# The low part of the transposed probabilities between the row maxima of two heads, in the first attention of a fused attention and mixture-of-experts kernel

## What is computed

```python
x = L0_attn_x
x = x + _layernorm(_L0_attn_ref(_layernorm(x, axis=-1), L0_attn_Wq, L0_attn_Wk, L0_attn_Wv, L0_attn_Wo), axis=-1)
x = x + _layernorm(_L0_ffn_ref(_layernorm(x, axis=-1), ...), axis=-1)

# in _L0_attn_ref
scores = jnp.einsum('bhqd,bhkd->bhqk', q, k) * scale
causal = jnp.tril(jnp.ones((T, T), dtype=bool))
scores = jnp.where(causal, scores, -jnp.inf)
attn = jax.nn.softmax(scores, axis=-1)
out = jnp.einsum('bhqk,bhkd->bhqd', attn, v)
out = out.transpose(0, 2, 1, 3).reshape(B, T, D)
return out @ Wo.T
```

## Time and profile before

| | |
|---|---|
| median of 3 runs | 939.19 us (936.19 to 939.78) |
| profiled execution, device time | 939.04 us |
| its span | 937.1 us |
| first attention, first scores to last projection | about 27.7 to 175 us of the span |
| busy in the whole span | PE 863.4 us (92%), DVE 616.3 (66%), ACT 567.0 (61%), POOL 456.4 (49%) |
| granted TensorE clock, mean | 0.98 of full speed |

### The profile page before, as it was taken

How to read it: one execution, slowest core, us unless ns; L and a number is a source line. 1 busy time by engine, 2 the same in 40 slices (tenths; PEclk the granted TensorE clock), 3 DMA queues, 4 the chain that set the end, 5 groups by cost and what they waited for, 6 DMA issues and landing times. The chain is left out here.

```text
span 937.1 us, 18767 instructions
## 1 busy us (share of the span) xinstructions
PE 863.4 (92%) x6108; PEld 799.0 (85%) x6108; DVE 616.3 (66%) x1620; ACT 567.0 (61%) x1570; POOL 456.4 (49%) x486
## 2 busy tenths in 40 slices
PE   5799997769999999999999999969999999999994
PEld 4699987668989989999889999858888888888884
DVE  5466768667787788877887777664545545454456
ACT  6889888656767776667676676654334343333333
POOL 3734334277677776677677777610222212222121
PEclk9999999998999999999999999997999999999997
DMA  7000000051124111411111111101433333333321
GB/s 238 1 22 27 22 23 1 23 147 35 34 61 122 47 40 40 136 46 45 36 35 46 45 37 47 41 1 41 150 107 102 116 117 100 112 101 117 118 79 45
DMA packets 50246, 63.34 MB, mean 68 GB/s; under 512 B 5728, under 2 KB 36064, under 8 KB 50176
## 3 DMA queue, kind: packets, MB, share of 16 engines
q1 hardware_dynamic: 49088, 61.41, 22.4%
q10 hardware_dynamic: 1088, 1.05, 0.3%
HBM read 41.86 MB, written 1.18 MB: 46 GB/s over the span
## 5 line engine op out<-in xcount | busy, mean ns | idle before, releaser
L639 POOL TENSOR_TENSOR b_prob<-b_prob,b_rsum 128x256 f32<-128x256 f32 (+1 forms) x128 | 104.8, 840 | 104.3 <-DVE b_rsum L621 104.3
L73 PE MATMUL banks<-act_t,b_w 128*128 128x256 f32 (+1 forms) x392 | 129.5, 330 | 4.4 <-DVE b_work L1203 3.3
L74 PE MATMUL banks<-act_t,b_w 128*128 128x256 f32 (+1 forms) x392 | 127.4, 325 | 0.0
L75 PE MATMUL banks<-act_t,b_w 128*128 128x256 f32 (+1 forms) x392 | 127.1, 324 | 0.0
L1965 ACT ACTIVATE moe_hid<-banks 128x512 fp32r<-128x512 f32 x66 | 39.5, 598 | 124.6 <-DVE banks L2056 124.6
L1364 ACT ACTIVATE b_prob<-banks,b_negmax 128x128 f32<-128x128 f32 (+1 forms) x256 | 103.6, 416 | 12.6 <-DVE b_negmax L1351 12.5
L2049 DVE TENSOR_TENSOR moe_gated<-banks,moe_share 128x512 f32<-128x512 f32 x66 | 45.6, 691 | 85.1 <-PE banks L75 81.2
L1220 ACT ACTIVATE b_qt<-b_work 128x512 fp32r<-128x512 f32 x64 | 40.5, 632 | 97.5 <-POOL b_work L1215 97.5
L1215 POOL TENSOR_TENSOR b_work<-b_work 128x512 f32<-128x512 f32 x64 | 88.1, 1377 | 9.2
L639 POOL TENSOR_TENSOR a_prob<-a_prob,a_rsum 128x256 f32<-128x256 f32 x64 | 52.4, 840 | 75.5 <-DVE a_rsum L621 75.3
L1211 POOL TENSOR_TENSOR b_work<-b_work,rope_t 128x512 f32<-128x512 f32 x64 | 83.2, 1299 | 7.2 <-DMA b_work<-b_work 7.2
(11 more groups left out here) (237 smaller groups left out, 3019.1 us busy)
## 6 DMA issues: line engine op xcount, KB each, us to landing
b_work<-b_work SPq DMA_DIRECT2D x128, 128.0 KB, 2.3
moe_share<-gates SPq DMA_DIRECT2D x32, 512.0 KB, 3.6
b_w_raw<-in_b_wq SPq DMA_DIRECT2D x4, 1024.0 KB, 5.5
b_w_raw<-in_b_wo SPq DMA_DIRECT2D x4, 1024.0 KB, 9.0
a_src_t<-act_t SPq DMA_DIRECT2D x5, 512.0 KB, 3.0
moe_w_raw<-in_wg SPq DMA_DIRECT2D x16, 128.0 KB, 2.1
moe_w_raw<-in_wu SPq DMA_DIRECT2D x16, 128.0 KB, 2.2
moe_w_raw<-in_wd SPq DMA_DIRECT2D x16, 128.0 KB, 2.2
```

What stands on the lines that cost most here:

```text
L73: nc.tensor.matmul(out, w_lo, m_hi, start=start, stop=False, skip_group_check=skip)
L74: nc.tensor.matmul(out, w_hi, m_lo, start=False, stop=False, skip_group_check=skip)
L75: return nc.tensor.matmul(out, w_hi, m_hi, start=False, stop=stop, skip_group_check=skip)
L639: last = self.m.nc.gpsimd.tensor_tensor(rows, rows, rsum[:, :, t:t + 1].to_broadcast([PART, 2, width]), ALU.mult)
```

## The change

The class of the first attention gets its own `slot_dve`. In it `dve_max` is called once per head, and `dve_prob_t` stands between the two calls. The calls that did nothing in this class (`dve_queries`, late units) are left out. Each call of `dve_max` has the wait on `exp_done` that was there once per slot. The second attention keeps the old `slot_dve`.

```diff
@@ -604,10 +604,10 @@
-    def dve_max(self, dve, p, P):
+    def dve_max(self, dve, p, P, heads=(0, 1)):
         nc, m = self.m.nc, self.m
         wait(dve, self.exp_done, 2 * P - 2)
-        for h in range(2):
+        for h in heads:
             wait(dve, self.s_full, 2 * P + 1 + h)
@@ -706,6 +706,28 @@
 class AttentionA(Attention):
+
+    def slot_dve(self, dve, it, p, units=True):
+
+
+        now = self.stage(it, p, 0)
+        if now:
+            self.dve_max(dve, *now[1:], heads=(0,))
+        if prob := self.stage(it, p, 3):
+            self.dve_prob_t(dve, *prob[1:])
+        if now:
+            self.dve_max(dve, *now[1:], heads=(1,))
+        if before := self.stage(it, p, 1):
+            self.dve_normalise(dve, *before[1:])
+        if out := self.stage(it, p, 4):
+            self.dve_outputs(dve, *out)
+        u = self.early_unit(p, units)
+        if u is not None:
+            self.dve_unit(dve, it + 1, u)
+        if now and p == PAIRS - 1:
+            self.dve_values(dve, it)
+        if p == 0 and not (isinstance(it, int) and it < 2):
+            self.dve_add(dve, it - 2)
```

## The result

The changed kernel takes 942.47 us (median of 11 runs, 940.85 to 947.25) against 939.04 for the kernel before beside it. The ratio is 1.0056, its 95% interval 1.0043 to 1.007: slower by 5.3 us (4.0 to 6.6), an interval that also holds the 4.7 us under which no change can be told. The two medians by themselves lie 3.4 us apart. Forecast were 5.45 us and 944.7 us, in a range of 941.4 to 948.4. The profiled execution took 942.47 us.

What follows compares the result with a forecast made beforehand. TensorE was taken to bound the first attention's middle, with something else at its end. Filling 0.5, iterations 3.15 and end 1.8 sum to +5.45 us over 939.04: 944.5, forecast as a 944.7 us median, range 941.4 to 948.4.

Steps and rivals of the forecast that it cites:

- a loop of VectorE and ScalarE: Steady middle of the first attention: the lengthened loop takes 17.31 us per iteration against TensorE's 16.46; chance 0.78.
- Full cover: Rival: the middle stays bound by TensorE, only filling and end cost 0.5 + 1.8, 941.5 us; chance 0.12.
- No effect: Rival: the low part L645 still runs when it did, since something else released it, 939.2 us; chance 0.02.
- the term of +3.15: Iterations 2 to 5 in the middle: 0.6 us for the first, then three of 0.85.
- the 0.26: First of iterations 2 to 5: ScalarE's wait at TensorE, 0.26 us, is used up before the full 0.85 shows.
- The end: Behind the loop: head 1's exponentials about 0.6 us later in slots 25, 26 and 31, together +1.8 us.
- my division by slots: Behind the loop: +0.59 in slot 25, repeated in 26, nothing in 27 to 30, +0.60 in slot 31.
- The filling: Slots 3 to 7: head 1's exponentials start 0.49 us later and pass it on in full, +0.5 us.
- L645 starts at 40.92 as before, because it had waited for L582: In the filling: the low part gets no earlier start, so head 1's exponentials move from 42.01 to 42.50.
- The extra waits: Each slot's added wait on `exp_done`, plus a register instruction in the loop's 16 slots: taken as nothing, at most +2.7 us.
- Faster: Rival: behind the loop L520 is released earlier eight times by 0.53 us, −4.2, so 935.0 us; chance 0.05.
- VectorE holds longer: Rival: in the new order VectorE's instructions hold their whole duration, 1.3 us more per iteration, 951 us; chance 0.03.

Runs made afterwards that it cites:

- e1: The kernel before with head maxima in two calls, old order, so only the extra wait and register instruction are added; ratio 0.9991 to before.
- e2: The change's new order only in iterations 0 to 5, iterations 6 and 7 as in the kernel before; ratio 1.0035 to before.
- e3: The change's new order only in iterations 6 and 7, the others as in the kernel before; ratio 1.0016 to before.
- e6: The change, with VectorE's add L654 moved ahead of the unit in slot p = 0; middle 66.64 us, ratio 1.0037 to before.
- e4: The change, but with the low part L645 ahead of both heads' maxima; middle 76.40 us, ratio 1.0203 to before.
- e10: The change itself measured and profiled once more, against the kernel before; middle 68.32 us, ratio 1.0052.
- e5: The change with L645 split: 384 columns between the two heads' maxima, 384 behind them; middle 66.50 us, ratio 1.0002 to before.
- e7: The kernel before with add L654 ahead of the unit and LayerNorm statistics of slots 24 and 25 moved into gaps; ratio 0.9981.
- e8: The kernel before, old order, with only add L654 moved ahead of the unit; end 52.20 us, ratio 0.9983.

## Why the prediction was right

The mechanism that was forecast is the one that the runs show. That the total of 5.45 us lies so near the 5.3 of the runs is in part luck: by the profiles the terms came out as −0.22, +2.50 and +2.01 where I had 0.5, 3.15 and 1.8.

- **The core, a loop of VectorE and ScalarE that outgrows TensorE's 16.46 us**: shown. e1 excludes the rest of the edit; e2 and e3 tie the middle's cost to the middle's order; e6 takes 0.60 out of the loop and 0.54 per iteration comes back, down almost to TensorE's own time; e4 puts more in and the iterations grow as summed. *Full cover* and *No effect* fall with the middle of 68.35.
- **Its size**: the term of +3.15 was too large, 2.50 measured. The iterations cost 0.27, 0.67, 0.90 and 0.66 where I had 0.6 and three times 0.85. The first counts for half of the difference; the pipeline seems to enter the loop with more slack than the 0.26 that I took from ScalarE's wait, which I didn't trace. For the others 17.31 was summed and 17.21 measured on average. The hand-over from the maxima to the exponentials is one reason (105.56 − 104.92 = 0.64 against my 0.71).
- **The end**: +1.8 forecast, +2.01 measured. Head 1's exponentials come 2.05 and 2.04 behind the first maximum (2.11 forecast) in slots 25 and 31. From slot 23 to slot 31 it is 39.11 us against 37.89, +1.22 for the 1.2 of slots 25 and 26; what follows is +0.79 for 0.6. But e2 shows that 0.7 of it belongs to the order in slot 23 and before, and e3, with the new order behind the loop alone, takes 38.41 us from slot 23 to slot 31, only 0.52 more than before. So my division by slots is right in its sum only, by luck.
- **The filling** was wrong: +0.5 forecast, −0.22 measured in the change's profile, −0.22 in e6's and −0.23 in e10's. The step that failed is "L645 starts at 40.92 as before, because it had waited for L582". It fits the profile that it was read from, but the block starts in one of two ways. In six profiles (the change, e2, e5, e6, e7, e10) its first scores come 7.2 to 7.4 us behind the block's first memset, in the other seven, the kernel before among them, 8.24 us. The eight matmuls just ahead of those scores, in e7, then in e8:

```profile
24.78 1.04 PE L826 MATMUL banks<-ident,b_w 128*128 128x128 f32 x8
```

```profile
25.33 1.91 PE L822 MATMUL banks<-ident,b_w 128*128 128x128 f32 x8
```

All six early profiles have 1.04 us there, all seven late ones 1.91 or 1.92. What decides it isn't known; the order of the low part doesn't, since e7 and e8 both have the old order in the filling. With the late start L645 does have to wait for L582: e4 puts it ahead of all maxima, and it starts 21.46 us behind the memset, against 21.50 before. With the early start L582 comes 0.58 us sooner (20.03 us behind the memset, against 20.61), and L645 can move. Kernel after, DVE and PE in the filling, answering:

```profile
39.69 0.95 DVE L645 TENSOR_TENSOR a_prob_t<-banks,a_prob_t 128x768 fp32r<-128x768 f32 x1
...
40.79 0.85 PE L520 MATMUL banks<-ident,a_prob 128*128 128x128 f32 x6 [0.50 <-DVE a_prob_t L645]
43.67 0.36 PE L73 MATMUL banks<-a_prob_t,b_w 128*128 128x256 f32 x1 [0.55 <-DVE b_w L920]
```

e7 has the old order there, and the same early start:

```profile
40.38 0.95 DVE L645 TENSOR_TENSOR a_prob_t<-banks,a_prob_t 128x768 fp32r<-128x768 f32 x1
...
41.47 0.85 PE L520 MATMUL banks<-ident,a_prob 128*128 128x128 f32 x6 [1.03 <-DVE a_prob_t L645]
43.80 0.36 PE L73 MATMUL banks<-a_prob_t,b_w 128*128 128x256 f32 x1 [0.35 <-DVE b_w L928]
```

Each block has to be counted from its own memset, 18.71 and 18.86. Then L645 is 0.54 us earlier with the new order and L520 0.53, because TensorE stood waiting for it. L73 starts at 24.96 against 24.94: it gains nothing, but it doesn't lose the forecast 0.5 either, because head 1's exponentials come at 22.49 against 22.46. ScalarE had the queries' copy and head 0's exponentials ahead of them in both. At slot 7 the change stands at 35.91 and e7 at 35.98. So against the same start the order gives 0.07 us back; the other 0.15 of the 0.22 come from the start. The change was not profiled with the late start.

- **The extra waits** were taken as nothing, with +2.7 as the upper end: e1's 65.81 against 65.85 us over 16 slots shows nothing. The Trainium skill ("Advanced Engine Details and Errata", Network/Comms) has 50 to 100 ns for a semaphore read, for which I had estimated 1.6 us more; the run disagrees, at least where the wait is already met and VectorE still works on the instruction before it.
- ***Faster*** failed where the prediction said it could: L520 was released earlier and waits 2.0 us less, but ScalarE waits for the maxima 33 times, for 15.2 us in all, where it had been 7 times and 3.8 us.
- ***VectorE holds longer*** failed too. In the new order 104.92 − 104.05 = 0.87 us lie between the starts of L645 and of the next maxima, for a duration of 0.95. The rule of the Trainium skill ("VectorE: DVE Perf Modes", The DRAIN you can't avoid), that the next operation waits for an empty pipe, isn't what these starts show. The same section adds that an operation which isn't held starts earlier, and the starts agree with that.

**What stays open.** The profiles give +4.3 us, the runs 5.3 (4.0 to 6.6) and 4.9 (3.6 to 6.2). The intervals hold the 4.3, but something beside the three parts may be left. The length of a single profile can't tell: what follows the first attention, which no edit touches, takes from 759.3 to 766.1 us in the thirteen profiles, a scatter larger than the effect. One candidate was seen and not settled, the granted clock in the filling. Windows of the change, then of e2:

```profile
30.00:35.00 5.00, 4.48 (x23) 3.64 (x22) 2.23 (x10) 3.88 (x16) 5.00 (x3) 0.71 0.00 0
```

```profile
35.00:40.00 5.00, 2.83 (x18) 2.32 (x18) 1.83 (x8) 3.59 (x14) 5.00 (x5) 0.83 0.02 3
40.00:45.00 5.00, 5.00 (x25) 4.78 (x23) 2.10 (x6) 3.25 (x11) 1.95 (x3) 0.50 0.00 0
```

In e2 TensorE was busy for 2.83 of 5 us and then ran at 0.50, the 1.2 GHz level. Its slot 7 came 1.6 us later than in the change, and that of e5 1.8 (0.57 in the same stretch). Such a dip stood in three of the six profiles with a changed order in the filling (the change, e2, e5) and in none of the seven with the old one. But all three also had the early start. Of the two profiles that separate these, e7 (early, old order) and e4 (late, changed order), neither had a dip. In the change's profile the dip cost nothing (35.91 against e10's 35.90 and e6's 35.91). So few profiles can't tell whether the order or the early start makes the dips likelier, nor how often the timed runs have them.

## What to carry to other kernels

The engine with the most waiting names the instruction it waits for, but moving that instruction forward in its queue moves another one back. Before doing so, follow the work that is passed over through every engine until the loop closes, and set that sum against the time of the bound engine: here 0.6 us per slot went into a loop that had 1.1 us per iteration to spare. Work that nobody waits for, like the add L654, is what should be moved, into the gaps of the same queue.

## What was not expected of the hardware

- TensorE's busy time can hide waits: e5's iterations are 0.16 us longer, and the two starts of L520 that cause it carry no bracket. The change's middle is 2.50 us longer, with 0.6 us of reported waits.
- The granted clock fell to 0.50 in a stretch of e2 in which TensorE was busy all the time, right behind one of 2.83 busy of 5.00. But from 30 to 35 us TensorE was busy for 2.81 of 5.00 in e8 and 2.77 in e4, and the clock stayed at 1.00 there and in the next 5 us. In the last part of the first attention 16.04 busy of 20.00 left it at 1.00 as well.
- The profile gives a granted clock of 1.00 from 25 to 30 us in both e7 and e8, and yet the same eight matmuls that start at 24.78 and 25.33 take 1.04 us in one and 1.91 in the other. It isn't only the modelled end of a matmul: ScalarE, which waits for the four matmuls ahead of them (24.28 and 24.43), starts 0.70 us behind their start in e7 and 1.15 in e8. The granted clock alone doesn't tell how fast TensorE works so early in the program.
